# Sparse graph attention, layers 1 to 3: the softmax worked out slot by slot with one-hot products

## The reference

```python
def layer(x, adj, W, a, alpha, bias, elu):
    wh = x @ W                                               # 4096 x 64
    e = (wh @ a[:64])[:, None] + (wh @ a[64:])[None, :]      # own term + neighbour's term
    e = where(e > 0, e, alpha * e)                           # alpha 0.2, 0.01, 0.2, 0.01
    att = softmax(where(adj > 0, e, -big), axis=1)
    y = att @ wh + bias                                      # a bias in layer 1 alone
    y = elu(y) if elu else y                                 # all but layer 1
    return layernorm(x + y)
```

## Time and profile before

| | us |
|---|---|
| median of three runs | 610.41 |
| span of the profiled execution | 608.0 |
| layer 0's last gather ends | 255.2 |
| first gathers of layers 1, 2, 3 | 289.61, 388.63, 489.48 |
| busy: PE, VectorE, ScalarE, GpSimd | 394.4, 366.7, 398.5, 282.3 |

### The profile page before, as it was taken

One profiled execution on the slowest core, in us unless ns is written; L12 is line 12 of the kernel. 1 busy time (PEld: TensorE's weight loads), 2 busy tenths in 40 slices (PEclk: granted clock), 3 DMA queues, 4 the chain that ended last, 5 costly groups with the idle time before them and its releaser, 6 DMA issues.

```text
span 608.0 us, 10701 instructions
## 1 busy us (share of the span) xinstructions
PE 394.4 (65%) x3404; PEld 321.7 (53%) x3404; DVE 366.7 (60%) x1696; ACT 398.5 (66%) x876; POOL 282.3 (46%) x296
## 2 busy tenths in 40 slices
PE   2165454443788548886627997755898876498773
PEld 1154333332576436865416886543787754397552
DVE  2104579965327898898321289854168984218996
ACT  3377876857437776696328588727588863858882
POOL 0000035746024234400777777377777467777710
PEclk9999999999999999999566999959899986899995
DMA  7998999969348861200221122122222113122210
GB/s 300 388 428 333 392 425 403 406 240 295 143 185 273 295 240 15 38 19 26 35 27 27 28 37 46 42 45 30 28 28 46 36 38 46 27 29 37 45 34 25
DMA packets 20547, 84.86 MB, mean 140 GB/s; under 512 B 6083, under 2 KB 11462, under 8 KB 16262
## 3 DMA queue, kind: packets, MB, share of 16 engines
q1 hardware_dynamic: 10102, 73.14, 30.7%
q0 software_dynamic: 9344, 9.89, 12.1%
q10 hardware_dynamic: 1040, 1.08, 0.5%
HBM read 78.72 MB, written 5.37 MB: 138 GB/s over the span
## 4 chain that ended last, share of the span: by engine, by line
DVE 29%; PE 20%; ACT 11%; issue 5%; POOL 3%; DMA 1%; ACTq 0%; DVEq 0%
PE bank L701 9%; DVE num L1252 4%; PE bank L686 4%; DVE arena L1221 3%; DVE x L1295 3%; POOL xg L525 3%; PE bank L669 3%; ACT arena L854 3%; ACT arena L840 3%; DVE stats L1277 3%; DVE lone L1238 2%; PE bank L667 2%; DVE mean_var L1280 2%; ACT arena L864 1%; ACT arena L828 1%
## 5 line engine op out<-in xcount | busy, mean ns | idle before, releaser
L525 POOL DMA_INDIRECT xg<-table,index x292 | 282.1, 966 | 298.2 <-DMA table<-wh 134.9
L828 ACT ACTIVATE arena<-arena,half 128x4096 bf16<-128x4096 int32 x31 | 114.5, 3701 | 18.8 <-DMA arena<-in_adj_t 18.3
L1221 DVE CUSTOM_DVE_ANT_0 arena<-bank,arena 128x256 f32<-128x256 f32 (+3 forms) x123 | 62.8, 521 | 101.3 <-ACT arena L840 101.2
L840 ACT ACTIVATE arena<-bank,sloped_own 128x256 f32<-128x256 f32 (+3 forms) x123 | 67.9, 556 | 53.1 <-PE bank L669 52.1
L701 PE MATMUL bank<-xg,arena 128*128 128x64 f32 x486 | 72.6, 284 | 24.3 <-ACT arena L864 22.6
L701 PEld LDWEIGHTS bank<-xg,arena 128*128 128x128 f32 x486 | 63.6, 197 | 35.3 <-ACT arena L864 31.2
L686 PE MATMUL bank<-packed,arena 128*128 128x128 f32 x339 | 64.7, 312 | 19.1 <-ACT arena L864 16.5
L1018 DVE MAX8 top<-bank 128x8 f32<-128x256 f32 x31 | 13.3, 430 | 84.4 <-PE bank L603 84.3
L669 PE MATMUL bank<-packed,xg 128*128 128x128 f32 x324 | 63.3, 298 | 0.0
L686 PEld LDWEIGHTS bank<-packed,arena 128*128 128x128 f32 x339 | 43.2, 158 | 30.8 <-ACT arena L854 25.6
L864 ACT COPY arena<-bank 128x256 f32<-128x256 f32 (+3 forms) x123 | 53.6, 443 | 6.8 <-PE bank L686 6.2
(11 more groups left out here) (141 smaller groups left out, 765.3 us busy)
## 6 DMA issues: line engine op xcount, KB each, us to landing
arena<-in_adj_t SPq DMA_DIRECT2D x31, 2048.0 KB, 11.0
xg<-table,index POOLq DMA_INDIRECT x292, 2.7
table<-wh SPq DMA_DIRECT2D x24, 132.0 KB, 1.7
arena<-in_adj SPq DMA_DIRECT2D x1, 2048.0 KB, 12.9
table<-wh ACTq DMA_DIRECT2D x1, 1056.0 KB, 25.7
x<-in_x SPq DMA_DIRECT2D x1, 1024.0 KB, 15.0
out_x<-x SPq DMA_DIRECT2D x8, 128.0 KB
packed<-in_c_packed SPq DMA_DIRECT2D x1, 306.0 KB
```

What stands on the lines that cost most here:

```text
L525: pool.indirect_dma_start(out=xg[:, c, :], out_offset=None, in_=table[l][0:rows, :], in_offset=bass.IndirectOffsetOnAxis(ap=index[:, c:c + ...
L828: nc.scalar.activation(masks[:, t % 2, :], arena[:, t % 3, :], ACT.Sign, bias=half[:, :]).then_inc(mask_made, 1)
L840: nc.scalar.activation(scores(l, n)[:, 0:m * P], score_ps[n % len(score_ps)][:, 0:m * P], ACT.Relu, bias=sloped_own[:, k:k + 1], scale=ALP ...
L1221: nc.vector.tensor_tensor_reduce(out=y, in0=score_ps[n % len(score_ps)][:, 0:m * P], in1=y, scale=-1.0, scalar=-FLOOR, op0=ALU.add, op1=AL ...
```

## The change

Layers 1 to 3 get rounds of their own, `later_round`, 26 a layer. The softmax of sparse tiles is no longer worked out in an array of rows by slots, but at the slots themselves:

- The gathered chunks are taken in 21 strips of three or four. PE transposes only the neighbour's terms (`spread_strip`), and VectorE takes from the bank, with a mask `slot_pen`, the largest term of each row of each tile (`most_of_strip`). The row's maximum is split in three bf16 parts (`split_most`), as is its own term (`split_own`, once a layer).
- PE brings both to the slots by one product a pair with `off_row`, which is now one-hot (`select`, six columns). VectorE works out for each slot how far its score lies under the row's maximum (`gaps`), ScalarE takes relu and exp of that (`weigh`), on 128 x 8 to 128 x 14 for a batch of tiles, and VectorE multiplies the gathered rows by it (`weigh_rows`).
- PE sums the weighted rows into the tiles' rows by one product a pair with a float32 table `one_hot`, whose 65th column is the softmax's divisor (`sum_slots`). GpSimd makes that table by 73 comparisons (128 x 128 or 128 x 256) after its last gather of layer 0 and before its first of layer 1.
- ScalarE divides (`divide`, four operations of 128 x 64) and scales the normalized rows (`scale_x`, four as well), which VectorE did; VectorE makes the factors (`divisors`, `scales`).
- The dense tile goes through the same stages as before, two segments a round in rounds 0 to 3 (mask) and 4 to 7 (exp, turn), and is summed in rounds 5 to 8.
- In the load stage a column with the number of the row is added to the lists (`row_no`, `row_id`): two more VectorE copies a batch. At the start of layer 1 VectorE passes twice over the mask's 10,368 columns.

The gathers and the writing of `table` are the same, but for the semaphores of the gathers, which count by strip. Each group's sums are taken by VectorE in rounds `SUMMED_AT` + 1; from group 3 on these are every second round, so that two rounds make one group.

The core of the diff, PE's order within a round and ScalarE's:

```diff
+            def later_round(l, i):                  # PE
+                for c in dense_at(i):
+                    spread_dense(l, c)
+                if strip_at(i) is not None:
+                    spread_strip(l, i)
+                for c in dense_at(i - DENSE_ROUNDS):
+                    turn_dense(l, c)
+                g = group_at(i - 2)
+                if g is not None and l < LAYERS - 1:
+                    turn_scaled(l, g)
+                b = batch_at(i - 1)
+                if b is not None:
+                    select(l, b)
+                for c in dense_at(i - DENSE_ROUNDS - 1):
+                    sum_dense(l, c)
+                b = batch_at(i - 2)
+                if b is not None:
+                    sum_slots(l, b)
+                if g is not None and l < LAYERS - 1:
+                    pe.wait_ge(sum_copied, l + 1)
+                    pe.wait_ge(selected_read, chosen(l, i))
+                    project_rows((l + 1) * GROUPS + g, l + 1)
...
+            def later_round(l, i):                  # ScalarE
+                g2 = group_at(i - 2)
+                if g2 is not None:
+                    scale_x(l, g2)
+                g = group_at(i - 1)
+                if g is not None:
+                    divide(l, g)
+                for c in dense_at(i):
+                    slope_dense(l, c)
+                for c in dense_at(i - DENSE_ROUNDS):
+                    exp_dense(l, c)
+                for c in dense_at(i - DENSE_ROUNDS):
+                    copy_dense(l, c)
+                if g2 is not None and l < LAYERS - 1:
+                    n = (l + 1) * GROUPS + g2
+                    copy_xt(n, n + 1)
+                b = batch_at(i - 1)
+                if b is not None:
+                    copy_terms(l, b)
+                if g is not None and ELU[l]:
+                    elu_later(l, g)
+                if b is not None:
+                    weigh(l, b)
+                if g is not None:
+                    estimate_rstd(g % 2, GROUP, -2.0, var_made, ln_made, rstd_made, group_n(l, g) + 1)
+                if g2 is not None and l < LAYERS - 1:
+                    copy_wh((l + 1) * GROUPS + g2, g2)
...
+            def most_of_strip(l, i):                # VectorE
...
+                    t = nc.vector.tensor_tensor_reduce(
+                        out=waste[:, n % 2, at:at + (hi - lo) * P], in0=score_ps[n % 2][:, (lo - c0) * P:(hi - c0) * P],
+                        in1=slot_pen[:, place * P:(place + hi - lo) * P], scale=1.0, scalar=FLOOR, op0=ALU.add, op1=ALU.max,
+                        accum_out=part_max[:, k, TILE_PARTS[k].index((lo, hi)):TILE_PARTS[k].index((lo, hi)) + 1])
+            def select(l, i):                       # PE
...
+                        t = nc.tensor.matmul(wh_ps[:, at:at + w], off_row[:, place:place + P], row_parts[:, k, :],
+                                             start=(k == tiles[0]), stop=(k == tiles[-1]))
+            def sum_slots(l, i):                    # PE
...
+                        t = nc.tensor.matmul(agg_ps[g % 2][:, at:at + F + 1], one_hot[:, place:place + P],
+                                             xg[:, c, 0:F + 1], start=(c == FIRST[k]),
+                                             stop=(c == FIRST[k] + CHUNKS[k] - 1))
...
+                t = nc.gpsimd.tensor_scalar(one_hot[:, PAIR0[c] * P:(PAIR0[c] + nt) * P],
+                                            slot_row[:, 1 + j0 * P:1 + (j0 + nt) * P], row_id[:, c:c + 1], None,
+                                            ALU.is_equal)
```

465 lines of the change are left out of this document (425 added, 40 removed).

## The result

The changed kernel takes 727.96 us (727.22 to 728.08), the kernel before 610.77 in the same runs: a ratio of 1.192, interval 1.190 to 1.194. The forecast was slower, 667 us, with a range up to 692. The direction was right, the size was not: 57 us were forecast on top of 610, 117 came. Its span is 726.0 us.

What follows compares the result with a forecast made beforehand. Queue order was taken to close a ring that sets each pair of layers 1 and 2. Strip 0 at 316.7, two periods 244.8, layer 3 100.2, output 2.7 and span to median 2.4 gave 667 us; range 614 to 692.

Steps and rivals of the forecast that it cites:

- I take a third of the way from high to low: TensorE's clock in layers 1 and 2: a period of 122.4 us, between 117.2 high and 132.9 low.
- GpSimd's tables: 73 comparisons before layer 1's gathers: 0.2 to 0.9 us each, cost 0 to +31 us, taken as 0.
- The ring: Layers 1 and 2: queue order makes each pair of rounds pay the whole chain, 10.6 us high clock, 13.5 low.
- The upper bound by the price of 64 columns: A pair at the higher clock, by the bounds of ScalarE's 128x64 operation: 10.1 to 11.5 us.
- The rival by which only VectorE's work counts: The ring does not close: 8.1 to 8.4 us a pair, 629 us in all, 612 to 640; chance 0.20.
- The lower sum: A period of layers 1 and 2 with TensorE at the lower clock: 132.9 us.
- its sums stand behind nothing: Layer 3, without turn and project: pairs go by VectorE's 8.1 us plus some 0.3; the layer 100.2 us.
- rival D: GpSimd's tables come late, above 0.47 us each, delaying layer 1's first gather: 675 to 697 us; chance 0.05.
- The passes over the mask: VectorE's two passes at the start of layer 1: 24 us in all, over by 315, cost nothing.
- They do not set the end: The next layer's first gathers: strip 0's are there and turned 26 us after leaving, no later than the ring.
- The early rounds: Rounds 1 to 13 after strip 0 is turned, layers 1 and 2: 10, 21.5 and 27.1, together 58.6 us.
- ScalarE's scaling: Four scalings of 128x64 a pair on ScalarE at 0.26 us each: 1.05 us, the same for four divisions.

Runs made afterwards that it cites:

- run 9: Changed kernel with slot sums ahead of the turn, gaps ahead of the residual, weighing ahead of statistics, projection and copy of `wh` at the next round's end; 697.5 us.
- Run 4: Changed kernel with 14 never-read products of 128x512 added on PE ahead of the turn of x, in each group round from round 10; 705.0 us.
- Run 12: Changed kernel with 24 never-read products of 128x512, instead of 14, on PE ahead of the turn of x; 706.1 us.
- run 13: Changed kernel with the last 28 of the 73 tables made by VectorE at the start of layer 1; 718.3 us.
- 14: Kernel of run 13 with the two passes over the mask's 10,368 columns made by ScalarE instead of VectorE; 712.7 us.
- run 7: Changed kernel with division and scaling of the rows put back on VectorE; 706.5 us.
- run 10: Kernel of run 9 with the dense scores ahead of strip 0 and the last 28 tables made by VectorE; 679.1 us.

## Why the prediction was right in direction and wrong in size

The step that failed is "I take a third of the way from high to low", TensorE's level in the periods, and beside it three terms that the sum put at nothing: GpSimd's tables, the dense tile's sums, and the ring of layer 3. Of the 61 us, 17 lie ahead of layer 1's strip 0, 33 in the two periods and 12 in layer 3.

**The ring: right in kind, closed by another way.** The order of queues read from the code gave 10.6 us a pair at the higher clock and 13.5 at the lower; the changed kernel has 12.5 to 13.2 at 0.50, the run with 24 products 10.1 to 11.4 at 1.00. (The upper bound by the price of 64 columns is 11.6, not 11.5.) At 1.00 some pairs have the chain that was forecast, with the copy of `wh` and the division. At 0.50 the steady pairs' chain goes from the projection through PE's next strip and its maxima, which the sum counts among VectorE's work and not in the ring. That the sum comes so near is in part luck: the strip's way is in the place of another of about its length, and the slot sums took 3.31 us, not 3.95. That it is the order, and not the work, is shown by run 9: 8.8 to 9.3 us a pair with the same operations. The rival by which only VectorE's work counts would have needed an order without a ring, and not even run 9 has that; VectorE's own work is 7.0 to 7.5 us a pair, where the sum had 8.1.

**The clock: the step that failed in the periods.** "I take a third of the way from high to low" was a choice between two sums; the pairs ran at 0.50 from end to end. The lower sum is itself too low: its 132.9 us a period have the last rounds at the lower clock, but the two and a half pairs of rounds 9 to 13 still at 10.6. With 13.5 there too it is 140.2, against 137.4 and 140.3 measured, and 705 us in all: so the clock was worth some 38 us of the 61, if the sum's other terms are taken as they stand. Run 4 bears the clock out: with products in the wait it rose, and 23 us went. Run 12 brought it to 1.00, but its products came into the chain themselves. The trace of before held a hint that I read the wrong way: at 0.50 PE stood after waits of up to 9.5 us, and a ring puts a wait in every pair.

**Layer 3: "its sums stand behind nothing" was wrong.** There too a ring closes, without the turn: weighing of the rows, slot sums (3.65 us at 677.61), PE's next strip (0.87), its maxima, residual, statistics, weighing. Pairs took 9.2 to 9.8 us with VectorE busy for 7.0 to 7.6 of them, where the sum had VectorE's 8.1 and 0.3.

**GpSimd's tables: the second step.** "Bounds 0.2 to 0.9 us each ... I take 0": the 128-column comparisons took 0.61 us, in the upper half of the bounds, against VectorE's 0.30 for the same operation in run 13. Groups by form of the changed kernel:

```profile
L644 POOL TENSOR_SCALAR arena<-slot_row,row_id 128x128 f32<-128x128 f16 x65 | 38.9, 611 | 0.1
...
L644 POOL TENSOR_SCALAR arena<-slot_row,row_id 128x256 f32<-128x256 f16 x8 | 13.0, 1621 | 0.0
```

So rival D happened, on top of the forecast: the tables took 51.7 us and the first gather left at 308.0, where it left at 292.0 to 294.1 in the runs that made 45 tables there. Of these some 15 us, some 9 are the comparisons' price (45.6 us without the stop that is told next, 0.62 each, as in the rival's 0.6). The row that I took as the nearest was another engine's. The Trainium skill's page "GPSIMD Engine Reference", section "4.1 Engine selection", calls one-input work there roughly even with VectorE; here it took twice VectorE's time, and the measurement decides.

**The passes over the mask: "nothing" was 6 us.** They were done well before strip 0, as worked out, and VectorE had no one waiting. But GpSimd stood still beside them (6.05 us of the 51.7), which no row of before could show. The Trainium skill's page "Perfetto Trace Analysis", section "Optimizing Scalar/DVE Operations", says that GpSimd and VectorE share a port that some VectorE operations hold for themselves; runs 13 and 14 agree, with 4.4 us that go when the passes leave VectorE.

**"They do not set the end": missing 3 to 4 us a layer.** Strip 0 needs two chunks that are not among the 17 early ones, and so the layer's last write. The chain above shows it: the write 1.72 us, two gathers, 2.42 to land, 0.90 to turn, 6.6 us from the copy of `wh` to strip 0, where the sum had 2.2 to 3.4.

**The early rounds: too cheap.** From strip 0 to the third group's statistics lie 62.7, 65.5 and 64.0 us; the sum had 58.6 in layers 1 and 2 and 53.1 in layer 3 to the end of round 13, in which these statistics stand. It has no term for the dense tile's sums (L915), which hold 6.8 to 8.4 us of each layer's chain of waits, and it gave 0.6 us to the larger batches' slot sums (L976), of which the first takes 6.40 us (30 passes) and the third 5.35 (24 passes). From layer 1:

```profile
350.10 3.31 PE bank L915 x16
353.41 6.40 PE bank L976 x30
```

With rounds 9 to 13 at the lower clock's price the sum is 65.9 in layers 1 and 2, so there pairs that are priced too high make up for the missing term; in layer 3 nothing does, and it is most of the 12 us.

**ScalarE's scaling: mis-sized, but small.** Four scalings took 1.41 us and four divisions 0.84 to 0.94, where the sum had 1.05 each. The estimate from the Trainium skill's page "ScalarE: Activation LUTs", section "What ACT_TABLE_LOAD costs", 1.4 and 1.1, was right on the scalings and high on the divisions. The point of that page's section "Rules for kernel authors", that multiplications belong on VectorE, held here for another reason than the price of an element: run 7 won 21 us, the larger part by the shorter way.

**Open.** With the ring made smaller, 28 of the tables off GpSimd and the dense scores ahead, 69 us over the kernel before remain (run 10). Two groups of these are seen: pairs of 9 us against 6.9, and 48 us from a layer's end to the first group's statistics, with PE in the chain (granted clock 0.75). What of the second is the clock and what the work was not told apart, and no run opens the ring.

## What to carry to other kernels

Before an array computation is replaced by a shorter one, draw the ring: follow one unit of work through every in-order queue and see whether an operation of unit n stands behind one of unit n-1 that waits for the end of unit n-2; if it does, the pace is the sum of the whole way and not the fullest engine, and moving work to an idle engine can make it worse, by 21 us here. Look for more than one way by which the ring closes: taking away one of them wins little while another is as long. TensorE's idle time had a second price here, since the work after the wait was done at half the clock; price a chain with such waits at the lower clock in all its parts. A free engine is a cover only at its own price for the operation: bound it by a factor, and ask what shares its way to memory.

## What the runs showed of the hardware that was not expected

- GpSimd takes 0.61 us for a comparison of 128x128 from f16 to f32, VectorE 0.30.
- Two VectorE passes of 2.86 to 3.04 us over 10,368 bf16 columns stop GpSimd, comparisons and DMA issue alike: two gathers took 3.11 and 3.16 us instead of 0.94. ScalarE's passes of the same size don't.
- Products that nobody reads, put in PE's waits, raised the granted clock from 0.50 to 0.64 to 1.00 and made a kernel with waits in its chain faster: 23 us of 728 in one, 3 us of 610 in the other.
